# Loading x by column and reordering the first half of an adapter, LayerNorm and mixture-of-experts kernel

## The reference

```
w1, w2 = W1[lang], W2[lang]                       # 128x32 and 32x128 for each batch
v  = x + relu(x @ w1 + b1[lang]) @ w2 + b2[lang]  # adapter
n  = layernorm(v) * gamma[lang] + beta[lang]
logits = n @ router_w.T                           # 8 experts
e, score = argmax(logits), sigmoid(max(logits))   # for each token
ns = n * score
moe = (silu(ns @ gate[e]) * (ns @ up[e])) @ down[e]
sh  = (silu(n @ shared_gate) * (n @ shared_up)) @ shared_down
out = x + moe + sh
```

## Time and profile before

| | us |
|---|---|
| median of 3 runs | 69.2 (68.46 to 69.24) |
| the profiled execution, its own time | 68.22 |
| its span, first to last instruction | 66.4 |
| busy: PE, weight loads of PE, DVE, ACT, POOL | 48.8, 36.4, 27.0, 22.7, 30.5 |
| POOL's 12 indirect DMAs to the output (L350) | 18.8 |
| POOL's 8 indirect DMAs to `slots_x` (L341) | 7.9 |
| DMA traffic | 8.05 MB |

### The profile page before, as it was taken

One profiled execution on the slowest core, in us unless ns is written; L12 is line 12 of the kernel. 1 busy time (PEld: TensorE's weight loads), 2 busy tenths in 40 slices (PEclk: granted clock), 3 DMA queues, 4 the chain that ended last, 5 costly groups with the idle time before them and its releaser, 6 DMA issues.

```text
span 66.4 us, 1128 instructions
## 1 busy us (share of the span) xinstructions
PE 48.8 (74%) x312; PEld 36.4 (55%) x312; DVE 27.0 (41%) x119; ACT 22.7 (34%) x65; POOL 30.5 (46%) x51
## 2 busy tenths in 40 slices
PE   3999999999898967999629999999999840000000
PEld 1376888676647424479414469999999730000000
DVE  2602364576881789747500433353333530000000
ACT  0640256568778081330023555533344200000000
POOL 4002950000138658860000000898888888898820
PEclk9999999999999999999999999999999999855555
DMA  0870899999899841111269590043421003424140
GB/s 0 255 267 4 141 336 163 114 176 239 370 402 427 363 149 62 47 40 45 77 158 238 126 314 11 0 40 33 40 27 7 5 4 24 40 22 40 9 37 2
DMA packets 7994, 8.05 MB, mean 121 GB/s; under 512 B 1161, under 2 KB 7187, under 8 KB 7732
## 3 DMA queue, kind: packets, MB, share of 16 engines
q1 hardware_dynamic: 5820, 6.74, 38.2%
q0 software_dynamic: 1984, 1.06, 11.9%
q10 hardware_dynamic: 184, 0.18, 1.0%
HBM read 5.40 MB, written 2.83 MB: 124 GB/s over the span
## 4 chain that ended last, share of the span: by engine, by line
PE 52%; POOL 10%; ACT 9%; DVE 7%; issue 7%; DMA 7%; POOLq 3%; ACTq 0%
PE bank L551 11%; POOL out_dram L350 9%; PE bank L575 8%; PE bank L547 6%; PE bank L365 6%; DMA slots_x<-x_rows,slot 4%; PE bank L379 4%; PE bank L395 3%; PE bank L389 3%; POOLq L47 3%; ACT x_rows L642 3%; DMA slot_x<-slots_x 3%; PE bank L373 2%; PE bank L539 2%; ACT L663 2%
## 5 line engine op out<-in xcount | busy, mean ns | idle before, releaser
L350 POOL DMA_INDIRECT out_dram<-y,slot_x x12 | 18.8, 1564 | 15.1 <-DVE y L949 12.4
L341 POOL DMA_INDIRECT slots_x<-x_rows,slot x8 | 7.9, 990 | 4.2 <-ACT x_rows L642 1.8
L448 PE MATMUL bank<-nT,sh_w 128*128 128x512 f32 (+1 forms) x20 | 8.3, 527 | 0.9 <-DVE hs L793 0.9
L944 DVE TENSOR_TENSOR eh<-eg,bank 128x256 f32<-128x256 f32 x12 | 5.0, 418 | 9.1 <-ACT eg L699 9.1
L551 PE MATMUL bank<-exT,ex_w 128*128 128x128 f32 x64 | 8.5, 275 | 0.0
L551 PEld LDWEIGHTS bank<-exT,ex_w 128*128 128x128 f32 x64 | 7.8, 192 | 0.0
L699 ACT ACTIVATE eg<-bank 128x256 f32<-128x256 f32 x12 | 4.6, 383 | 9.0 <-PE bank L551 6.5
L949 DVE COPY y<-bank 128x128 f32<-128x128 f32 x12 | 3.4, 287 | 4.8 <-PE bank L575 4.8
L575 PE MATMUL bank<-ex_w,eh 128*128 128x128 f32 x32 | 5.0, 278 | 0.5 <-DVE eh L944 0.5
L683 ACT ACTIVATE exT<-bank 128x128 f32<-128x128 f32 x12 | 3.2, 273 | 5.8 <-PE bank L539 5.8
L365 PE MATMUL bank<-warm 128*128 128x512 bf16 x11 | 4.4, 538 | 1.1 <-DVE eps L712 1.1
(11 more groups left out here) (125 smaller groups left out, 74.7 us busy)
## 6 DMA issues: line engine op xcount, KB each, us to landing
ex_w<-in_expert_w_dram SPq DMA_DIRECT2D x2, 1536.0 KB
slots_x<-empty_row SPq DMA_DIRECT2D x1, 967.5 KB, 11.3
slot_x<-slots_x SPq DMA_DIRECT2D x4, 129.0 KB, 3.8
x_tok<-in_x_dram SPq DMA_DIRECT2D x2, 256.0 KB, 3.6
out_dram<-r_rows SPq DMA_DIRECT2D x2, 256.0 KB, 3.2
sh_w<-in_shared_w_dram SPq DMA_DIRECT2D x1, 384.0 KB, 3.5
slot_x<-slots_x SPq DMA_DIRECT2D x4, 64.5 KB, 1.9
slot_x<-slots_x SPq DMA_DIRECT2D x1, 193.5 KB, 4.0
```

The lines of the kernel that those rows point to most:

```text
L341: nc.gpsimd.indirect_dma_start(out=slots_x, out_offset=bass.IndirectOffsetOnAxis(ap=slot[:, b:b + 1], axis=0), in_=x_rows[:, b, :], in_off ...
L350: nc.gpsimd.indirect_dma_start(out=out_rows, out_offset=bass.IndirectOffsetOnAxis(ap=slot_x[:, tile, H:H + 1].bitcast(U32), axis=0), in_=y ...
L448: last = nc.tensor.matmul(bank[SH_BANKS[k][u]][:, first * S:end * S], sh_w[:, u * FF + k * P:u * FF + (k + 1) * P], nT[:, g * GB + first:g ...
L944: nc.vector.tensor_tensor(eh[:, i % 3, :], eg[:, i % 2, :], bank[EX_GU[i % 2]][:, FF:2 * FF], ALU.mult).then_inc(run.eh_done, 1)
```

## The change

The host passes x a second time as `x_cols`, with features as rows, and SP loads it straight into `xT`. The eight transposes, the three copies to `xT` and their semaphores go. `start_v` multiplies `xT` by the identity, four matmuls in place of two. `x_tok` is used for the residual alone and is loaded later. The orders of SP, ACT, DVE and PE in the adapter and the norm change.

```diff
+            sp.dma_start(xT[:, 0:GB, :], x_cols[:, 0:GB, :]).then_inc(x_in[0], 16)
+            sp.dma_start(vec_rows[:], lang_vecs).then_inc(vec_in, 16)
             sp.dma_start(w2_all[:], w2b2).then_inc(w2_in, 16)
+            sp.dma_start(xT[:, GB:B, :], x_cols[:, GB:B, :]).then_inc(x_in[1], 16)
             sp.wait_ge(x_in[1], 16)
             sp.dma_start(sh_w[:], shared_w).then_inc(sh_in, 16)
...
             sp.wait_ge(sh_in, 16)
+            sp.dma_start(x_tok[:], x).then_inc(x_tok_in, 16)
             sp.dma_start(ex_w[:, 0:E // 2, :], expert_w[:, 0:E // 2, :]).then_inc(ex_in, 16)
```

```diff
+            def start_v(g):
+                pe.wait_ge(x_in[g], 16)
+                for b in range(g * GB, (g + 1) * GB):
+                    nc.tensor.matmul(v_place(b), xT[:, b, :], ident[:], start=(b % GB < 2), stop=False,
+                                     skip_group_check=True)
...
-            keep_warm(WARM, 7)
+            keep_warm(WARM, 6)
             pe.wait_ge(pool_const, 2)
-            turn_tokens(0)
             start_v(0)
...
             adapter_down(0)
-            turn_tokens(1)
             pe.wait_ge(w2_in, 16)
             pe.wait_ge(dve_const, 1)
             for b in PAIRS[0:GB]:
                 adapter_up(b)
+            pe.wait_ge(x_in[1], 16)
+            pe.wait_ge(hT_act, 2)
+            pe.wait_ge(hT_dve, 2)
             adapter_down(1)
             pe.wait_ge(params_done, 2)
             start_v(1)
-            for b in PAIRS[GB:B]:
+            for b in PAIRS[GB:GB + 2]:
                 adapter_up(b)
-            keep_warm(1, 2)
-            for b in range(GB):
+            for b in PAIRS[0:GB]:
                 turn_z(b)
+            for b in PAIRS[GB + 2:B]:
+                adapter_up(b)
...
-            keep_warm(TABLE, 2)
             router(0)
```

On ACT:

```diff
-            act.wait_ge(xT_ps, 1)
-            nc.scalar.activation(xT[:, 0:2, :], bank[X_T[0]][:, 0:2 * S], ACT.Copy).then_inc(xT_act, 1)
             act.wait_ge(params_done, 1)
             relu(0)
             relu(2)
-            act.wait_ge(xT_ps, 4)
-            nc.scalar.activation(xT[:, GB:B, :], bank[X_T[2]][:], ACT.Copy).then_inc(xT_act, 1)
-            for b in PAIRS[GB:B]:
-                relu(b)
+            relu(4)
             deviation(0)
+            relu(6)
             normalize(1)
             normalize(3)
             act.wait_ge(params_done, 2)
             affine(1)
-            affine(2)
             affine(3)
             deviation(1)
...
             half_tanhs(0)
-            for b in range(GB):
-                scale_rows(b)
             normalize(5)
+            scale_rows(0)
             normalize(7)
+            scale_rows(1)
+            scale_rows(2)
+            scale_rows(3)
             affine(5)
             affine(7)
```

More of the change, by code:

```diff
@@ L15, with adaln_moe_kernel @@
 LN_EPS = 1e-5
-def adaln_moe_kernel(nc, x, ids, w1rw, w2b2, lang_vecs, shared_w, expert_w, out):
+def adaln_moe_kernel(nc, x, x_cols, ids, w1rw, w2b2, lang_vecs, shared_w, expert_w, out):
     S, B, H = x.shape
@@ L133, in adaln_moe_kernel @@
         y = sb("y", [P, TILES, H])
-        x_in = [sem(f"x_in{i}") for i in range(GROUPS)]
+        x_in, x_tok_in = [sem(f"x_in{i}") for i in range(GROUPS)], sem("x_tok_in")
         ids_in, vec_in, w1_in, w2_in = sem("ids_in"), sem("vec_in"), sem("w1_in"), sem("w2_in")
@@ L191, in adaln_moe_kernel @@
         N_ROWS, NUM, TABLE = 6, 2, 3
-        X_T = (0, 1, 0, 0)
         SH_BANKS = [(0, 1), (7, 5)]
@@ L219, in sh_y_place @@
             return bank[SH_Y[b % len(SH_Y)]][:, 0:H]
[L221 to L224, removed]
+        HT_ACT = (0, 2, 4, 6)
+        HT_DVE = (1, 3, 5, 7)
+        NT_DVE = (0, 2, 4, 6)
+        NT_ACT = (1, 3, 5, 7)
         def relu_done(b):
             return (hT_dve, HT_DVE.index(b) + 1) if b in HT_DVE else (hT_act, HT_ACT.index(b) + 1)
-        Z_ORDER = (0, 1, 2, 3, 4, 6, 5, 7)
+        Z_ORDER = PAIRS
         def zT_ready(b):
@@ L366, in keep_warm @@
                                      start=True, stop=True)
-            def turn_tokens(g):
+            def start_v(g):
                 pe.wait_ge(x_in[g], 16)
                 for b in range(g * GB, (g + 1) * GB):
[L371 to L380, removed]
+                    nc.tensor.matmul(v_place(b), xT[:, b, :], ident[:], start=(b % GB < 2), stop=False,
+                                     skip_group_check=True)
             def adapter_down(g):
                 for b in PAIRS[g * GB:(g + 1) * GB]:
[L384 to L387, removed]
                     pe.wait_ge(w1_odd if b % 2 else w1_even, b // 2 + 1)
@@ L403, in turn_z @@
                     pe.wait_ge(*z_done(7))
+                if b == 3:
+                    pe.wait_ge(*relu_done(7))
                 if b == 4:
@@ L430, in _ @@
             start_v(1)
-            for b in PAIRS[GB:B]:
+            for b in PAIRS[GB:GB + 2]:
                 adapter_up(b)
-            keep_warm(1, 2)
-            for b in range(GB):
+            for b in PAIRS[0:GB]:
                 turn_z(b)
+            for b in PAIRS[GB + 2:B]:
+                adapter_up(b)
             def router(g):
-                for b in range(g * GB, (g + 1) * GB):
+                for b in PAIRS[g * GB:(g + 1) * GB]:
                     pe.wait_ge(*nT_done(b))
@@ L764, in _ @@
             select_w1(3)
-            dve.wait_ge(xT_ps, 2)
-            nc.vector.tensor_copy(xT[:, 2:GB, :], bank[X_T[1]][:, 0:2 * S]).then_inc(xT_dve, 1)
             dve.wait_ge(params_ps, 1)
@@ L778, in _ @@
                 mean_var(b)
+            relu(5)
+            relu(7)
             deviation(0)
@@ L783, in _ @@
             affine(0)
+            affine(2)
             for b in PAIRS[GB:B]:
@@ L797, in residual @@
                 dve.wait_ge(sd_ps, b + 1)
+                dve.wait_ge(x_tok_in, 16)
                 nc.vector.tensor_tensor(r_rows[:, b, :], sh_y_place(b), x_tok[:, b, :], ALU.add).then_inc(r_done, 1)
@@ L863, in _ @@
             find_home_hot(0)
+            bias_of_z(1)
             find_over_n(0)
             find_place_hot(0)
-            bias_of_z(1)
             find_at_home(0)
@@ L973 @@
         "x": a["x"].transpose(1, 0, 2),
+        "x_cols": a["x"].transpose(2, 0, 1),
         "ids": a["itok_B_0_8"],
```

4 lines of the change are left out of this document (removed).

## The result

The changed kernel took 68.49 us, median of 20 executions (67.92 to 75.61), against 68.86 (68.17 to 69.82) of the kernel before beside it: ratio 0.9925 [0.9896, 0.9954], faster by 0.75%. The profiled execution took 68.0 us, its span 66.3 (before 68.22 and 66.4). On a second chip six executions had a median of 67.08 against 67.93, ratio 0.9793 [0.9716, 0.9869]. Seven of the 20 executions of the changed kernel took 70 to 76 us (none of the kernel before did), and the ratios leave such disturbed ones out; with them its mean is 70.1 against 68.9.

What follows compares the result with a forecast made beforehand. Slots were taken to gate POOL's scatters, with a fixed length behind the eighth. Gating by the fill gives 0.3 us, the fifth scatter 0.3: profiled 68.22 to 67.6, median forecast 68.5, range 67.0 to 69.4.

Steps and rivals of the forecast that it cites:

- The gate changes from slots to fill: First scatter on POOL: would wait for the fill at 17.95 instead of group 0's slots at 18.27, gaining 0.3 us.
- The fifth scatter's idle of 0.30: POOL's fifth scatter would no longer wait for group 1's slots, showing the usual 0.30 idle and gaining 0.3 us.
- the slack of the fill: Before the first scatter: the fill landed at 17.55, only 0.72 us ahead of group 0's slots at 18.27.
- the shift d: Landing of SP's second half of x, delaying the fill equally: between -1.05 and +0.95 us, taken as +0.4.
- `adapter_down`: Group 0 on PE: its first start would move from 7.20 to about 6.5, 0.7 us sooner, after w1 at 6.18.
- The warm pairs' removal: PE in group 0: dropping two pairs of warm matmuls, against group 1's remaining `adapter_up` work, would gain 0.4 us.
- everything behind the eighth scatter is one fixed length: From the eighth scatter to the end: unchanged length, so 0.6 us gained at that scatter would reach the end whole.
- has to spare: PE behind the eighth scatter: y of the first tile ready at 39.13, 1.3 us before the stores land at 40.4.
- loads 5.3: SP behind the eighth scatter: issuing the nine slot loads would still take 5.3 us.
- C: Rival: PE runs group 0 at the slow clock after idling, slots at 19 to 19.6, median 69.6 to 70.2; 5%.

Runs made afterwards that it cites:

- after_5: The changed kernel unedited, timed again on a second chip: median 67.08 us against 67.93 of the kernel before, ratio 0.9793.
- xtok_last: The changed kernel with x_tok loaded behind both loads of the experts' weights: median 66.98 us against 67.97 of the kernel before.
- warm_back: The changed kernel with the five removed warm matmuls put back: 68.37 us against 68.47 of the kernel before, ratio 0.9867.
- x1_second: The changed kernel with the second half of x issued second, not fourth, on SP's queue: median 66.81 us against 67.93 of the kernel before.
- before_cold: The kernel before without the same five warm matmuls: 69.25 to 69.88 us in five of six executions, 67.55 in one, against 68.47.
- before_pe_shift: The kernel before with three of seven warm matmuls replaced by 24 tiny ones: 67.73 us against 67.93, ratio 1.0003.
- second profile: A second profiled execution of the unedited changed kernel, on another chip: 65.87 us against a median of 67.97 of the kernel before.
- x1_warm: The changed kernel with the second half of x issued second and the five warm matmuls put back: 68.42 us against 68.47, ratio 0.9932.

## Why the prediction was right, and where it was not

**The result is inside it**: 68.5 forecast, 68.49 measured, profiled 67.6 forecast and 68.0 measured; about 2% counts as no change, and the ratio on the first chip is 0.75%, on the second at the edge (2.1%, interval 1.3 to 2.8%). That agreement is partly luck, as the steps show: two terms of the gate were mis-sized against each other, and behind the eighth scatter a gain and a loss that nobody forecast cancelled in the profiled execution.

**Right, and shown.** The gate changes from slots to fill, so most of the 1.96 us that group 0 won (18.27 to 16.31) does not arrive. Behind the fill's landing the first scatter started after 0.85 us in both profiles of the changed kernel, and in after_5 (0.87), xtok_last (0.90) and warm_back (0.86); forecast was 1.0. The place of the second half of x on SP's queue counts, which was the prediction's reason for the upper part of its bounds: in second place instead of fourth (x1_second against after_5, on one chip) this 256 KB load was issued 0.78 us sooner and took 3.2 us instead of 3.9, and the fill was issued 1.54 us sooner. The fifth scatter's idle of 0.30 came as forecast, where the clock held.

**Right by luck: the slack of the fill and the shift d.** Against the one profile that the prediction had, d was +0.53 for +0.4. But in that profile the second half of x took 4.6 us. In before_cold and before_pe_shift, with the same loads in the same order, it took 3.8 and 3.0, and SP could issue the fill at 5.49 and 4.71, not at 6.25, while the changed kernel issues it at 6.39 to 6.78 in four profiles:

```profile
4.71 0.43 SPq L261 DMA_DIRECT2D slots_x<-empty_row  x1
```

So d is some 0.9 to 2.1 us (1.7 between before_pe_shift and after_5, on one chip), mostly above the bound of 0.95, and the slack was 2.2 us in before_pe_shift (fill 15.61, slots 17.81), not 0.72. The two errors cancel: on that chip the first scatter moved from 18.80 to 18.46 (after_5), by the 0.3 of the forecast.

**Mis-sized, harmless.** `adapter_down` started 0.5 us sooner than forecast, since w1 was there by 5.58 and not 6.18; the slots still came at 16.31, so these 0.5 us were lost again, 0.4 of them ahead of the statistics (8.07 for 8.2). The warm pairs' removal was priced at 0.4; warm_back, with them, takes 8.82 us from the statistics to the slots (8.65 to 17.47) where the first profile takes 8.24, so it was worth 0.6.

**The step that failed**: "everything behind the eighth scatter is one fixed length", and so "moves as a block". It does not. In the first profile the block's start came 0.63 us sooner (31.28 to 30.65). The slot loads were 1.02 shorter, the stores took 3.9 us instead of 3.4 to land, and the last landed at about 39.4 (34.97 + 0.52 + 3.9), 1.0 sooner than the 40.4 worked out from the earlier trace rows. All of that was lost at tile 0, whose y came 1.24 us later than before (39.13 to 40.37) and used up the 1.3 us that PE "has to spare". The output DMA follows y by 0.95 us, and ends where it did: 61.88 against 61.93. The slack was counted as if PE's own work stood still, though it hangs on DVE's products and on the clock. In the second profile, without the standstill, the same block was shorter by 1.2 us (28.67 to 41.37 is 12.70, 27.54 to 39.08 is 11.54).

The term that made it shorter is "loads 5.3". The nine slot loads took 4.27 to 4.48 in all ten profiles of the changed kernel and its variants, and 5.30 to 5.53 in three of the four of the kernel before and its variants. Two profiles of one chip, before_pe_shift (67.53 us) and after_5 (66.78), show its weight: the eighth scatter starts at 28.23 and 28.22, the loads take 5.45 and 4.28, the first output DMA starts at 40.79 and 40.11. There the reordered first half gained nothing (0.3 us at the first scatter, lost again at the fifth, where the clock had fallen), and the loads that nobody had touched gained 0.7 us.

**The rival that was priced too low**: C, at 5%. It put the fall into group 0 because of an idle time from 5.7 to 6.5 that hardly occurred (0.20 us ahead of 5.33). The fall came elsewhere: near 16 to 19 in three profiles that keep the new PE order (after_5, xtok_last, x1_second), costing 0.4 to 1.3 us at the fifth scatter, and at 31.5 to 34.8 in the first profile, where standstill and fall together cost 1.0 at the output. The five warm matmuls were counted as time to be had. before_cold prices them as a guard: without them the kernel before was 0.8 to 1.4 us slower in five of six executions. The fall varies from execution to execution of one kernel: of the changed kernel's three profiles one has it at 31.5 to 34.8, one near 16 to 19 and one nowhere ahead of its tail, and of the six executions of before_cold one has the mean clock of the kernel before (0.932, which lies in that kernel's 0.916 to 0.943 on the same chip) and five have less (0.860 to 0.901).

**Where the gain is.** The execution profiled with neither standstill nor fall is some 2 us faster than the kernel before, 65.87 against 67.97, and about half of that is the slot loads. The best of xtok_last (65.71) and of x1_second (64.94, against 67.93) had a mean clock as high (0.935 and 0.944, against 0.930), but were not profiled. On the first chip none of the 20 executions was below 67.92. **Open**: what DVE waits for in the standstill; how often it occurs in unprofiled executions; what makes those of 74 to 76 us (four of the 20, with a mean clock of 0.936 to 0.944, above the 0.926 that none of those under 69 us exceeds, so it is not the half clock); and whether an instruction fetch of PE causes SP's slow load. No version tried is clearly better than the changed kernel: on its chip the lowest median, x1_second's 66.81 against 67.08, lies well inside the spread of both, and warm_back, at 0.9867 of the kernel before on its chip, overlaps the changed kernel's two ratios.

## What to carry to other kernels

When a gate is removed, read the second-latest arrival at the same wait: here it was 0.72 us behind, so 2 us of faster work could give only a fraction. Read it in several executions: in another one it was 2.2 us behind, because a load landed sooner. A stretch called fixed is fixed only while all that meets in it keeps its order; write down the second chain's slack and what that chain itself hangs on. Don't book warm matmuls as free time: take them out alone first and look at the granted clock in several executions, since one profile shows only one outcome.

## What the hardware showed that was not expected

- The granted clock fell from 1.00 to 0.50 in after_5 at the end of a stretch in which PE was busy for 1.65 of 2.00 us (14 to 16), and did not fall in the first two profiles of the same kernel, with 1.65 and 1.66. In the earlier trace rows PE was busy for only 1.06 of 2.00 us, and the clock stayed at 1.00.
- DVE stood still for 2.1 to 2.2 us on a releaser that the trace does not know in the first profile, warm_back and x1_warm. Each time it resumed within 0.1 us of SP's first slot load, that is of the landing of the eighth scatter (30.65 and 30.65, 30.23 and 30.16, 29.95 and 29.94). x_tok isn't what it waited for: it had landed by 19.0 (issued at 10.03, 9.0 us), and in two of the three the waiting instruction is the product `hs`. In warm_back ACT had stood still too, for 2.96 us up to 29.43, and `hs` needs what it then wrote (done at 30.03): the standstill is not one of DVE alone.
- Where the fill is issued matters to others: from ACT, beside the first loads, it took 8.8 us instead of 11.3 in the kernel before, and 9.7 instead of 11.1 to 11.5 in the changed one, while the shared weights took 7.5 us instead of 3.5 in the first and 6.3 instead of 3.6 in the second, where PE was then busy for only 0.34 of the 2.00 us from 5 to 7.
